# Reordering one round of a windowed-attention pipeline: projection first on TensorE, values one unit ahead

## The reference

```
x = x + L0(groupnorm(x))      # ZCA whitening in 16 groups of 4 channels, then weight and bias
x = x + L1(groupnorm(x))      # attention in windows

# L1, on xn = batchnorm(groupnorm(x)):
tok  = 7x7 = 49 positions of a window (strided by 8), 64 channels each; 64 windows an image
qk   = tok @ qk_w.T           # 128 columns; reshaped to (-1, 49, 2, 16, 16): q and k of 16 heads
attn = softmax(q k^T * 0.25)  # 49 x 49 for each head
v    = relu(tok @ v_w.T)
out  = attn @ v, put back to (16, 64, 56, 56)
```

## Time and profile before

| | |
|---|---|
| median of three runs | 568.25 us |
| the profiled execution | 567.16 us |
| span in its trace | 565.4 us |
| PE busy | 467.5 us (83%) |
| PE's weight loads busy | 350.7 us (62%) |
| DVE busy | 333.3 us (59%) |
| ACT busy | 293.8 us (52%) |
| POOL busy | 193.2 us (34%) |
| chain that ended last: DMA diag, SPq L235, PE L812, ACT L357 | 19%, 15%, 10%, 8% |
| granted PE clock, mean | 0.933 of full |

### The profile page before, as it was taken

One profiled execution on the slowest core, in us unless ns is written; L12 is line 12 of the kernel. 1 busy time (PEld: TensorE's weight loads), 2 busy tenths in 40 slices (PEclk: granted clock), 3 DMA queues, 4 the chain that ended last, 5 costly groups with the idle time before them and its releaser, 6 DMA issues.

```text
span 565.4 us, 40427 instructions
## 1 busy us (share of the span) xinstructions
PE 467.5 (83%) x18274; PEld 350.7 (62%) x18274; DVE 333.3 (59%) x1079; ACT 293.8 (52%) x514; POOL 193.2 (34%) x159
## 2 busy tenths in 40 slices
PE   6689950897578897998998999899989989989982
PEld 5457740622356676676776767667767767767762
DVE  5523348786135465666566666666666656756762
ACT  1113220165444565665766666666666666666650
POOL 8300000002103333354344445445434434534432
PEclk9679985699589899999999999999999999999997
DMA  8940000000111141341314234131432413243232
GB/s 317 422 181 5 5 3 1 0 1 1 60 60 60 51 124 59 113 121 72 121 57 128 77 108 128 72 114 71 128 98 76 138 59 114 78 122 106 86 95 58
DMA packets 30645, 52.18 MB, mean 92 GB/s; under 512 B 5248, under 2 KB 20096, under 8 KB 29696
## 3 DMA queue, kind: packets, MB, share of 16 engines
q1 hardware_dynamic: 30592, 51.50, 26.7%
HBM read 12.95 MB, written 12.85 MB: 46 GB/s over the span
## 4 chain that ended last, share of the span: by engine, by line
PE 39%; DMA 19%; SPq 15%; ACT 9%; DVE 7%; issue 7%; POOL 1%; POOLq 0%; DVEq 0%; ACTq 0%
DMA diag<-qk_all 19%; SPq L235 15%; PE ps L812 10%; ACT qk_all L357 8%; PE ps L725 6%; PE ps L840 5%; PE ps L784 4%; PE ps L737 4%; PE ps L865 3%; PE ps L901 2%; PE ps L887 2%; ACT vst L365 1%; PE ps L825 1%; DVE X L583 1%; DVE dupm L413 1%
## 5 line engine op out<-in xcount | busy, mean ns | idle before, releaser
L660 DVE TENSOR_REDUCE rmax<-ps 113x16 bf16<-113x784 f32 x128 | 124.8, 975 | 158.7 <-PE ps L840 158.6
L303 POOL TENSOR_TENSOR X<-X,otok 128x392 f32<-128x392 f32 x64 | 108.6, 1697 | 228.8 <-DVE otok L693 228.8
L350 ACT ACTIVATE prob<-ps 113x784 f32<-113x784 f32 x128 | 105.6, 825 | 80.6 <-PE ps L872 79.1
L865 PE MATMUL ps<-diag,qk_all 64*49 64x98 f32 x4096 | 130.8, 248 | 6.8 <-issue 6.2
L365 ACT ACTIVATE vst<-ps 49x256 f32<-49x256 f32 x256 | 96.9, 379 | 46.2 <-PE ps L901 41.6
L297 POOL TENSOR_SCALAR xs<-X,affined 128x392 f32<-128x392 f32 x64 | 70.2, 1097 | 135.7 <-DVE affined L651 117.3
L872 PE MATMUL ps<-mdiag,sel 64*49 64x98 bf16 x2048 | 111.5, 203 | 0.0
L865 PEld LDWEIGHTS ps<-diag,qk_all 64*49 64x49 f32 x4096 | 99.5, 122 | 12.3 <-issue 9.6
L840 PE MATMUL ps<-diag,qk_all 64*49 64x196 bf16 x1024 | 49.4, 266 | 33.9 <-DMA diag<-qk_all 32.6
L357 ACT ACTIVATE qk_all<-ps 128x784 f32<-128x784 f32 x64 | 52.8, 825 | 31.1 <-PE ps L812 31.1
L887 PEld LDWEIGHTS ps<-prob,ones 113*32 113x32 f32 x2048 | 43.8, 110 | 38.8 <-issue 38.7
(11 more groups left out here) (162 smaller groups left out, 411.1 us busy)
## 6 DMA issues: line engine op xcount, KB each, us to landing
diag<-qk_all SPq DMA_DIRECT2D x256, 98.0 KB, 2.0
out<-X SPq DMA_DIRECT2D x32, 392.0 KB, 4.2
X<-x_in SPq DMA_DIRECT2D x7, 1024.0 KB, 15.2
X<-x_in SPq DMA_DIRECT2D x7, 544.0 KB, 16.0
X<-x_in SPq DMA_DIRECT2D x4, 256.0 KB, 3.8
X<-x_in SPq DMA_DIRECT2D x2, 192.0 KB, 4.9
X<-x_in SPq DMA_DIRECT2D x1, 160.0 KB, 4.9
wqk<-w_qk SPq DMA_DIRECT2D x1, 64.0 KB, 17.4
```

Of the source, the lines that this page charges most:

```text
L303: g.tensor_tensor(rows_of(u), rows_of(u), otok[u % 2][:].rearrange("p k a s -> p k s a"), ALU.add).then_inc(S["x_ready"], 1)
L350: a.activation(prob[u % 3][0:ROW, k].rearrange("p h g x j q -> p h (g x j q)"), ps[0:ROW, B_ST:B_ST + 2, 0:8 * POS], ACT.Exp, scale=SCALE) ...
L660: v.tensor_reduce(rmax[u % 3][0:ROW, :, 8 * k:8 * k + 8], ps[0:ROW, B_S:B_S + 2, 0:8 * POS].rearrange("p h (v q) -> p h v q", q=POS), AX.X ...
L865: mm(ps[64 * e:64 * e + POS, B_ST + hh, col:col + 2 * POS], qk[u % 3][r, g, k, 2 + x_, :], diag[u % 3][r, e::2, g, k, x_, :], start=True, ...
```

## The change

- **PE**: a round begins with project_qk(w), then scores_for_exp(u, 0), scores_for_max(s, 0), project_v(s) in place of project_v(w), sum_weights(z), scores_for_max(s, 1), scores_for_exp(u, 1), weigh_values(z), turn_max(s).
- **ACT**: keep_qk(w), weights(u, 0), keep_v(s), weights(u, 1).
- **DVE**: maximum(s, 0), invert(z), maximum(s, 1), spread_max(s), broadcast(z), divide(z). The division is in the round of its own unit's sums and no longer a round later.
- **POOL**: normalise(i + 3), add(i - 1).
- **Waits**: v_ready has a credit of 2 in place of 1, since the values are now one unit ahead; project_qk(1) also waits for the first qk_ready, and the last project_v for v_ready, where the running number does not fit.

```diff
-        CREDIT = {"v_ready": 1, "prob0": 2, ...
+        CREDIT = {"v_ready": 2, "prob0": 2, ...
...
-            for i in range(-3, UNITS + 2):
+            for i in range(-3, UNITS + 1):
                 if has(i + 3):
                     normalise(i + 3)
-                if has(i - 2):
-                    add(i - 2)
+                if has(i - 1):
+                    add(i - 1)
...
                 u, w = i, i + 2
-                if has(u):
-                    weights(u, 0)
                 if has(w):
                     keep_qk(w)
                 if has(u):
+                    weights(u, 0)
+                if has(i + 1):
+                    keep_v(i + 1)
+                if has(u):
                     weights(u, 1)
-                if has(w):
-                    keep_v(w)
...
-            for i in range(-1, UNITS + 2):
+            for i in range(-1, UNITS + 1):
                 s, z = i + 1, i - 1
                 if has(s):
                     maximum(s, 0)
-                if has(z - 1):
-                    divide(z - 1)
-                if has(s):
-                    maximum(s, 1)
                 if has(z):
                     invert(z)
                 if has(s):
+                    maximum(s, 1)
                     spread_max(s)
                 if has(z):
                     broadcast(z)
+                    divide(z)
...
                 need("v_ready", at)
+                if u == 1:
+                    pe.wait_ge(S["qk_ready"], 1)
...
-                need("qk_ready", at)
+                if u < UNITS - 1:
+                    need("qk_ready", at)
+                else:
+                    pe.wait_ge(S["v_ready"], UNITS - 1 + CREDIT["v_ready"])
...
                 u, s, w, z = i, i + 1, i + 2, i - 1
+                if has(w):
+                    project_qk(w, at)
                 if has(u):
                     scores_for_exp(u, 0, at)
                 if has(s):
                     scores_for_max(s, 0, at, landed)
-                if has(w):
-                    project_qk(w, at)
+                    project_v(s, at)
                 if has(z):
                     sum_weights(z, at)
                 if has(s):
                     scores_for_max(s, 1, at, landed)
                 if has(u):
                     scores_for_exp(u, 1, at)
-                if has(w):
-                    project_v(w, at)
+                if has(z):
+                    weigh_values(z, at)
                 if has(s):
                     turn_max(s, at)
-                if has(z):
-                    weigh_values(z, at)
```

More of the change, by code:

```diff
@@ L194, in conv_preact_kernel @@
         load = [sem(f"load{n}") for n in range(len(PIECES))]
-        CREDIT = {"v_ready": 1, "prob0": 2, "prob1": 3, "max0": 1, "max1": 1, "mdiag_ready": 2, "rden_ready": 4, "o_ready": 4}
+        CREDIT = {"v_ready": 2, "prob0": 2, "prob1": 3, "max0": 1, "max1": 1, "mdiag_ready": 2, "rden_ready": 4, "o_ready": 4}
         diag_in = [S["diag0"], S["diag1"], S["diag2"]]
```

## The result

The changed kernel takes 534.98 us (median of four runs, 532.63 to 536.41) against 569.28 us for the kernel before in the same series. The ratio is 0.9411, with a 95% interval from 0.9356 to 0.9466: 34 us less, where the prediction had 50. The time lies just inside the upper end of the range; the gain is two thirds of the forecast.

What follows compares the result with a forecast made beforehand. The prediction took the trip from qk copy through diag DMAs to the next projection as the bound. Savings of 39.1 (steady rounds), 11 (start) and 1 (end), less 1 for reading error, made 50: 568.25 to 518 us, range 508 to 535.

Steps and rivals of the forecast that it cites:

- diag trip: qk copy, diag DMAs, landing, scores, next projection: said to set the 6.03 us round, with 1.3 slack after the change.
- The back edge: PE's loop jump every third round: 0.36 us, no longer covered by the DMA wait, so 0.12 a round.
- The start: First eight rounds, 60.94 us before: 11 us saved, with bounds of 4.8 and 15.
- the four stalls that it kept: Stalls inside weigh_values in the early rounds, 1.97, 0.98, 0.93 and 1.22 us, assumed to remain.
- The slower rival: GpSimd delivers xs late to project_qk at the round's head: round 6.7 us, kernel 601 us; chance 0.05.
- the term 5.43 for a round: Steady round after the change: PE's list of 5.31 plus 0.12 for the back edge, if no wait comes late.
- Which waits come late after the change: Step checking each wait in the new round: none late, smallest slacks 0 to 0.06 us, 0.02 a round added.
- PE's own list, the new floor: Step adding the times of PE's groups in a round, read from the old order: 5.31 us.
- the sign that the prediction gave for its failure as a whole: PE's groups taking longer in the new order, for instance project_qk before scores_for_exp; no size given.
- the end: From the last copy of qk to the span's end, 25.7 us: 1 us saved, between 0 and 3.
- DVE's second maximum leads: Rival: turn_max waits for the second maximum behind invert(z); round 5.68 us, kernel 533 us; chance 0.22.
- the fetch at each back edge: Rival: PE's instructions are fetched anew at 19 loop jumps, 16 us more, kernel 534 us; chance 0.03.

Runs made afterwards that it cites:

- after_one_spread: The changed kernel with one of a unit's four diag DMAs issued and three left out: 530.77 us, ratio 0.9403.
- sums_before_values: The changed kernel with sum_weights(z) moved ahead of project_v(s) on PE: 523.18 us, ratio 0.9232.
- v_wait_moved: The changed kernel with the wait for v_ready moved from the head of project_qk to ahead of weigh_values: 527.22 us, ratio 0.9289.
- max_before_invert: The changed kernel with DVE's second maximum put back before the inversion of the sums: 534.57 us, ratio 0.9449.
- xs_wait_moved: The changed kernel with the wait for xs moved from the head of project_qk to just ahead of turn_max: 537.07 us, ratio 0.9488.
- halves_and_xs_wait: The changed kernel with sums before values, maximum before inversion, turn_max between weigh_values' halves, xs wait ahead of turn_max: 518.77 us, ratio 0.9170.

## Why the prediction was right about the trip and wrong about the round

**Right.** The diag trip left the path: no wait for it in the steady rounds, and after_one_spread gains nothing. The copy of qk was to be at PE 1.92 after the round's start; it was (381.68 - 379.76). The back edge was to cost 0.36; it costs 5.92 - 5.54 = 0.38, and PE's loop is not refetched. The start gave 9.1 for 11, but partly by a granted clock of 0.93 for 0.80, which the prediction didn't have, and the four stalls that it kept gave way to seven others. The slower rival did not come: divide ends at 381.39, 1.63 into the round, 0.2 ahead of forecast.

**Wrong: the term 5.43 for a round, 55 times.** It was 5.674, which is 13 us of the 19 by which the saving in the traces, 30.7, falls short of 50. The step that failed is "Which waits come late after the change". It let two waits on PE cost nothing, and they cost 0.36 a round together:

- project_v for the copy of qk, 0.16 to 0.17, where the prediction had a slack of 0.05. The copy was on time, but PE came early: at 0.68 + 0.86 + 0.21 = 1.75 and not at 1.97. Shown by sums_before_values (5.35).
- The waits at the head of project_qk, now right behind turn_max, 0.19. The prediction had slacks of 0.8 and 0.5 there, and the waits were indeed met in time; I had taken a wait that is already met for free wherever it stands. Shown by v_wait_moved (5.36).

The step before it, "PE's own list, the new floor", was off the other way, by 0.13, and hid a part of this. Each distance was read with its old neighbour behind it and taken for the step's own. Without the two waits the new list would be 0.68 + 0.86 + 0.21 + 0.59 + 0.82 + 0.21 + 0.96 + 0.71 + 0.14 = 5.18, and not 5.31. Where a group of 64-row tiles is followed by one of 113-row tiles, or the other way round, the distance is longer: project_qk takes 0.82 ahead of such a change and 0.68 without, weigh_values 0.84 and 0.71, scores_for_exp 0.96 and 0.86, turn_max 0.14 and 0.07. The changes have moved to other groups. (project_v's 0.59 for 0.54 is not of this kind, since it had 113-row tiles behind it before too; its cause stays open.) So the sign that the prediction gave for its failure as a whole, PE's groups taking longer in the new order, came true for single groups and not for their sum.

5.18 + 0.17 + 0.19 = 5.54. No run has both waits out of the way in this order, so the 5.18 is a sum of distances and not a measured round.

**Wrong by size: the end**, -3.6 for +1. I left the stalls of the written-out rounds out there. They come 3.8 to 3.9 us apart (before 3.6 and 3.9). PE goes through these rounds faster now, and the fetching seems to keep its pace; that this turned 2.5 us of stall into 5.1 is read from two traces and was not tested alone.

**The rival with the same time was not the cause.** "DVE's second maximum leads" gave 533, next to what was measured, and turn_max did start just when the maximum allowed (384.97 against 384.82 + 0.14). max_before_invert took the maximum out of its way and the time stayed. That 534.98 lies within the range is luck: the upper end of 535 was drawn for this rival and for the fetch at each back edge, and neither came.

**Missed without harm: the second loop.** "A round lasts as long as the trip" was true, but the values' copy made a loop of the same 6.03, and the profile named only the one that came last. The change opens both. Had it only moved the projection, a reckoning that knew the diag trip alone would have given rounds of 5.5 where the run gave 7.48 and more.

**The back-edge fetch.** The Trainium skill's page Runtime: NRT & Kernel Launch, Instruction fetch mechanics, gives PE's instruction memory as 2048 instructions. Three rounds of 504 matmuls and loads are 1512, six are 3024; the traces agree, with 30 packets against 162. The page calls the cost of a block boundary mostly hidden; the six-round run, at 8 us and more a round for 5.54, does not agree, even though a part of that is the lower clock.

## What to carry to other kernels

When one wait is removed, look for a second chain of the same length: cut the first one's cost by itself and see whether the round moves. A distance between two groups belongs to the pair and not to the first group, so a reordered list must be added up with its new neighbours, and a slack of 0.05 us found by such adding is no slack. Put waits ahead of long groups, not around a group of a few instructions, and keep a loop's body small enough that it is fetched once. Before a saving is put down to an edit, compare the granted clock of the two stretches.

## What the runs showed of the hardware that was not expected

- A met wait costs 0.19 us on PE next to a group of 4 matmuls (xs_wait_moved), 0.06 to 0.07 next to 32 (halves_and_xs_wait), and nothing ahead of 64 (v_wait_moved).
- Where groups of 64-row and 113-row tiles follow each other, the distance between their starts is 0.07 to 0.14 us longer (turn_max 0.14 against 0.07, project_qk 0.82 against 0.68, weigh_values 0.84 against 0.71).
- PE's loop body of three rounds runs at 5.54 us a round once held, with no instruction packet in 300 us. One of six is fetched in each pass, at 8 us a round and more, part of it at a lower granted clock, and with 4.4 us idle at a back edge.
